# The order of GpSimd's gathers and row additions in a mixture of experts: weights, then rows, then the additions of two tiles back

## The reference

```python
h = _rmsnorm(x, rms_weight)
ht = h.reshape(-1, d)                       # 2048 rows of 512
probs = jax.nn.softmax(ht @ router_w, axis=-1)
topv, topi = jax.lax.top_k(probs, K)        # K = 2
topv = topv / jnp.sum(topv, axis=-1, keepdims=True)
g = jnp.einsum('td,edf->tef', ht, w_gate)   # 8 experts, f = 256
u = jnp.einsum('td,edf->tef', ht, w_up)
eo = jnp.einsum('tef,efd->ted', jax.nn.silu(g) * u, w_down)
moe = jnp.einsum('te,ted->td', w_dense, eo)
sh = jax.nn.silu(ht @ sw_gate) * (ht @ sw_up) @ sw_down
return (moe + sh).reshape(b, s, d)
```

## Time and profile before

| | |
|---|---|
| median of 3 runs | 2080.37 us (2079.14 to 2083.13) |
| the profiled execution, its own time | 2080.4 us |
| its span, first to last instruction | 2078.6 us |
| TensorE busy | 1999.9 us, 96% |
| GpSimd busy | 686.8 us, 33% |
| software DMA queue q0 (all of GpSimd's gathers and additions) | 56.64 MB |
| granted TensorE clock, mean | 0.987 of full speed |

### The profile page before, as it was taken

The page is one execution under the profiler, slowest core; times in us unless marked ns, Lnnn a source line. Parts: engine busy times, 40 slices in busy tenths (PEclk is TensorE's granted clock), DMA queues, the critical chain, the costliest instruction groups (busy, mean ns, idle before and its releaser), DMA issues. The chain is left out here.

```text
span 2078.6 us, 29478 instructions
## 1 busy us (share of the span) xinstructions
PE 1999.9 (96%) x11805; PEld 1587.9 (76%) x11805; DVE 944.5 (45%) x1555; ACT 766.9 (37%) x1210; POOL 686.8 (33%) x652
## 2 busy tenths in 40 slices
PE   6988999999999999999999999999999999999997
PEld 4776687788888888888888888666666667898886
DVE  6775433212222222222222255777667655765554
ACT  5464612112112122121221212465556564266565
POOL 5444301010111111111111147446453333346664
PEclk9998999999999999999999999999999999999999
DMA  5242200103021030010100003644444320178884
GB/s 195 76 132 87 72 1 26 41 1 122 21 85 58 1 122 21 21 41 1 41 20 21 26 1 74 156 98 91 91 97 86 75 100 31 74 245 238 237 239 133
DMA packets 91335, 171.31 MB, mean 82 GB/s; under 512 B 10864, under 2 KB 35952, under 8 KB 88240
## 3 DMA queue, kind: packets, MB, share of 16 engines
q1 hardware_dynamic: 77584, 112.79, 18.7%
q0 software_dynamic: 13616, 56.64, 9.5%
HBM read 131.51 MB, written 54.13 MB: 89 GB/s over the span
## 5 line engine op out<-in xcount | busy, mean ns | idle before, releaser
L1570 POOL TENSOR_TENSOR ML<-MT,MH 128x512 fp32r<-128x512 f32 x128 | 165.0, 1293 | 791.3 <-ACT MH L1372 791.1
L1514 DVE SCALAR_TENSOR_TENSOR X<-PS,WT,X 128x512 f32<-128x512 f32 x128 | 96.0, 750 | 391.0 <-PE PS L57 390.5
L1372 ACT ACTIVATE MH<-MT 128x512 fp32r<-128x512 f32 x128 | 80.9, 632 | 512.4 <-DVE MT L1441 512.4
L55 PE MATMUL PS<-HH,Wg0h 128*128 128x512 f32 x512 | 200.5, 392 | 0.1
L55 PE MATMUL PS<-Wd0h,MH 128*128 128x512 f32 x512 | 199.6, 390 | 0.1
L56 PE MATMUL PS<-HL,Wg0h 128*128 128x512 f32 x512 | 199.7, 390 | 0.0
L57 PE MATMUL PS<-HH,Wg0l 128*128 128x512 f32 x512 | 199.6, 390 | 0.0
L55 PE MATMUL PS<-HH,Wu0h 128*128 128x512 f32 x512 | 199.5, 390 | 0.0
L57 PE MATMUL PS<-HH,Wu0l 128*128 128x512 f32 x512 | 199.3, 389 | 0.0
L56 PE MATMUL PS<-HL,Wu0h 128*128 128x512 f32 x512 | 199.3, 389 | 0.0
L56 PE MATMUL PS<-Wd0l,MH 128*128 128x512 f32 x512 | 199.2, 389 | 0.0
(11 more groups left out here) (482 smaller groups left out, 4317.2 us busy)
## 6 DMA issues: line engine op xcount, KB each, us to landing
HH<-Kd SPq DMA_DIRECT2D x48, 256.0 KB, 4.2
HL<-Qd SPq DMA_DIRECT2D x48, 256.0 KB, 6.4
STG<-in_Wg SPq DMA_DIRECT2D x8, 1024.0 KB, 5.2
STG<-in_Wu SPq DMA_DIRECT2D x8, 1024.0 KB, 5.2
STG<-in_Wd SPq DMA_DIRECT2D x8, 1024.0 KB, 5.3
X<-in_x SPq DMA_DIRECT2D x16, 256.0 KB, 7.8
Vd<-VO SPq DMA_DIRECT2D x16, 256.0 KB, 2.0
Kd<-KH SPq DMA_DIRECT2D x16, 256.0 KB, 2.3
```

The lines of the kernel that those rows point to most:

```text
L55: e.matmul(out_, a_[0], b_[0], start=start, stop=False)
L1372: e.activation(M[0][:, f, :], MT[i % 2][:, :], ACT.Copy).then_inc(m_h, 1)
L1514: e.scalar_tensor_tensor(X[:, k, :], PS[:, bank["d", 4 * n + q], :], WT[:, k, x:x + 1], X[:, k, :], ALU.mult, ALU.add).then_inc(d_x, 1)
L1570: e.tensor_tensor(M[1][:, f, :], MT[i % 2][:, :], M[0][:, f, :].bitcast(f32), ALU.subtract).then_inc(m_l, 1)
```

## The change

GpSimd's loop is reordered. In step i the weights of job(i)+2 are asked for first, then the rows of tile i+2, and last the additions, of the tile two steps back instead of one. Two tiles' additions are left behind the loop instead of one. No instruction is added or removed, and no wait; PE, DVE, ACT and SP have the same instructions in the same order.

```diff
             for i in range(R0, N):
+                if job(i) + 2 <= NR:
+                    gather_weights(e, job(i) + 2)
                 if i + 2 < N:
                     gather_tile(e, i + 2)
-                if job(i) + 2 <= NR:
-                    gather_weights(e, job(i) + 2)
-                if i > R0:
-                    add_rows(e, i - 1 - R0)
-            add_rows(e, NR - 1)
+                if i > R0 + 1:
+                    add_rows(e, i - 2 - R0)
+            for t in (NR - 2, NR - 1):
+                add_rows(e, t)
             e.wait_ge(added, 32 * NR)
```

## The result

The changed kernel takes 2076.14 us (median of 17 runs, 2073.38 to 2079.33) beside 2082.34 us for the kernel before in as many runs on the same chips: a ratio of 0.9967, 95% interval 0.9960 to 0.9974. It is faster by 0.33%, some 7 us where 13.7 were forecast.

The account below looks back on a forecast made before the run. TensorE was taken to wait for late weights in a loop through GpSimd and the DMA queue. 17 x (10.55 - 9.7) = 14.4 us, less 0.7, gives 13.7 off 2080.4: 2067 us, range 2059 to 2081.

Parts of the forecast that it names:

- What bounds the kernel before: Routed stage: TensorE waits for late weights, in a loop through GpSimd and the DMA queue; at most 20.2 us to gain.
- Weights: GpSimd's weight issue moves from 7.7 to 3.1 us after a step's first gate matmul; all stalls for `W1g` should go.
- Rows: Row gathers, now queued behind 1.5 MB of weights, have 9.14 us from the weights' issue until the next step's transposes.
- L = 9.8: Landing time in us of rows, from the weights' issue, that fits the forecast step of 9.7 us.
- The DMA engines: Expected new bound in the routed steps: about 9.2 us of work each, so 9.7 us steps, saving 14.4 us over 17.
- full pace: Rival: rows land in time, as in the one instance of 8.1 us; all 20.2 us come, 2060 us; chance 0.12.
- The formula: At the transposes, each step stalls by s = (L - 9.14)/2, L being the rows' landing time from the weights' issue.
- Steps 8 to 12: Early routed steps, at 9.36 us before, now have rows behind weights: charged 0.15 us for 5 steps, 0.7 us.
- The end: Last additions, of tiles 29 and 30, keep the same order as before: no change in time.
- The additions' wait for each other: On GpSimd, each addition needs the one before complete; claimed 1.5 us to spare, so not a bound.
- the handed-over gain: Rival: rows late by as much as weights were, break-even at L = 11.0, 2080 us; chance 0.15.
- The slower one: Rival: rows behind weights stall 1.4 us a step at L2406, stage 11 us slower, 2091 us; chance 0.15.

Follow-up runs that it names:

- e7: Changed kernel with rows asked for one tile earlier (tile i+3) and additions of one tile back instead of two: 2062.52 us, 0.9904 of the kernel before.
- e8: e7 with rows and weights exchanged, so rows of tile i+3 go out ahead of the weights: 2083.87 us, 1.0003 of the kernel before.
- e4: Changed kernel with additions of two tiles back put ahead of the rows, so rows come last: 2109.04 us, 1.0112 of the kernel before.
- e1: Changed kernel with rows put back ahead of weights, keeping only the additions' two-tile lag: 2071.11 us, 0.9934 of the kernel before.
- e2: Changed kernel with additions of one tile back again, keeping weights ahead of rows: 2112.47 us, 1.0132 of the kernel before.

## Why the prediction was right or wrong

- **What bounds the kernel before** was right: weights late behind `OB`, additions and rows. e7 takes the whole 20 us by issuing weights ahead of rows, and e8 loses it by the exchange alone.
- **Weights** were right: out 3.4 us after the gate instead of 7.7 (one round; from step 10 on it was 7.5 to 10.4), and no wait for them is left. I had 3.1, from steps 8 and 9. From the end of step 9 on ScalarE writes two `OB` just before `W1d`, which is the likely reason and was not tried. It took 0.26 us from the rows' budget.
- **Rows** were the right place for the new stall. The budget was 8.9, not 9.14. L = 9.8 was chosen by way of the DMA engines' share; the late rows measured 9.4 to 11.2.
- **The DMA engines** is the step that failed: "here I expect the new bound", 9.2 us of work at a share of 0.96, so steps of 9.7 us and a term of 14.4 us. The 17 steps took 10.08 us each, and the term measured 8.0. Nor did full engines set that. e7 has the same load, and its window of tiles 13 to 30 is the counterpart of the earlier trace rows. The work by this measure is 0.93 x 9.37 = 8.7 us a step, not 9.2: a share summed over a stretch with stalls was read as a demand. It is not far off, though. Without its last step, which asks for no weights, e7 runs at 0.96 and still in steps of 9.37 us, so the engines are nearly full, but they do not stop that pace; e4 is far slower at 0.75. I expected a share near 0.95 with the change, and it is 0.86. What held the steps instead was the order in the queue: rows behind weights, with 8.9 us to land.
- **Luck.** The bound that was wrong brought the number nearer. By the one instance of the new order, 8.1 us, my forecast would have been full pace, 2060 us.
- **The formula** s = (L - 9.14)/2 took L as the same in every step and left out the clock. I had 5.8 us for what the 17 steps exceed 159.1 by; it measured 12.2. Of these TensorE stands for 8.3 and is busy for 3.9 longer, of which 1.7 went to the lower clock behind a stall of 2.1 us. I had read that effect in the earlier trace rows and not carried it into the new stall.
- **Steps 8 to 12** were charged 0.7 us and lost 1.3 (46.8 to 48.1).
- **The end** was set to nothing and lost 1.3 us: additions of two tiles back leave a chain of additions that wait for each other. Every run with that lag and its data has 24.2 us or more there, except e4 with 23.1, and every other 22.8 to 23.1.
- **The additions' wait for each other** was judged harmless, with 1.5 us to spare. It held GpSimd for 10.8 us, in four places, mostly at the end. In e1 it was the thing that mattered.
- **Rivals.** The result lies between my forecast and the handed-over gain. The slower one, rows behind weights with L = 12, is what e4 became, with 11.5 to 14.1; e2 is as slow by its shorter budget.

Term by term for the profile: 8.0 less 1.3 and 1.3 is 5.4 us, and the timed medians differ by 6.2.

## What to carry to other kernels

For each transfer in a shared queue write down when it may be issued, when its data is wanted, and what lies ahead of it; moving one forward takes the time from the next, and the latter may have the shorter budget. Before reordering, look whether a buffer is free a whole step sooner: here the slack was there for the asking, and took the stage to TensorE's pace. A DMA share measured in a stretch with stalls does not tell how much the engines can carry.

## What the runs showed of the hardware that was not expected

The busy time of the DMA engines for nearly the same transfers depends on their order: 0.84 x 226.1 = 190 us in the 22 steps before, 0.83 x 219.4 = 182 after, 0.89 x 206.1 = 183 in e7. Single steps of e7 show shares up to 1.03, so the measure is not exact to a few per cent.

Two kernels with equal instructions and bytes, e4 and e7, differ by 47 us in the stage, and a third of that is clock and not waiting. In the stage of all these runs every stall of TensorE of 3 us or more was followed by 1.4 to 3 us lost at the lower granted clock, and none of under 2 us was. Of those between, some were (2.1 us after the change, 2.3 in e4) and some not (2.8 in e4; in e2 one of 2.85 was and another was not), and no run tells why.

GpSimd's issue of one addition, 1.6 us in the earlier trace rows, took 2.0 to 2.7 us in many places after the change, and 2.4 in two places before it; what held it there was not tried.
